# Attention on one NeuronCore: mixing on four array quadrants in the banks of the output, and another order of a round

## The reference, cut to what matters

```python
x = x + conv(group_norm(x))
x = x + attention(group_norm(x))

def attention(x):                       # n tokens, 8 heads of 16 channels
    q, k, v = x @ Wq.T, x @ Wk.T, 2 * (x @ Wv.T)
    q, k, v_h = l2norm(q), l2norm(k), l2norm(v)      # per head
    A = softmax(einsum('bnhd,bngd->bnhg', v_h, v_h))  # 8 x 8 per token, over g
    q = einsum('bnhg,bngd->bnhd', A, q)
    k = einsum('bnhg,bngd->bnhd', A, k)
    P = softmax(einsum('bnhd,bnhe->bnde', k, q))      # 16 x 16 per token, over e
    out = einsum('bnhd,bnde->bnhe', v, P)
    # transposed and reshaped to (n, 128), so that a row mixes tokens of one image
    return out @ proj_w.T + proj_b
```

## Time and profile before

| what | value |
|---|---|
| median of three runs | 3333.34 us |
| the profiled execution | 3327.52 us, span 3325.7 us |
| TensorE matmuls busy | 2987.1 us, 90% of the span |
| weight loads busy (beside matmuls) | 2207.7 us, 66% |
| VectorE, ScalarE, POOL busy | 1866.8, 1275.8, 570.3 us |
| mean granted TensorE clock | 0.955 |
| four attention bursts on the chain that ended last | logits 7%, mixing, scores and outputs 6% each |

### The profile page before, as it was taken

How to read it: one execution, slowest core, us unless ns; L and a number is a source line. 1 busy time by engine, 2 the same in 40 slices (tenths; PEclk the granted TensorE clock), 3 DMA queues, 4 the chain that set the end, 5 groups by cost and what they waited for, 6 DMA issues and landing times. The chain is left out here.

```text
span 3325.7 us, 143922 instructions
## 1 busy us (share of the span) xinstructions
PE 2987.1 (90%) x62769; PEld 2207.7 (66%) x62769; DVE 1866.8 (56%) x3334; ACT 1275.8 (38%) x2841; POOL 570.3 (17%) x419
## 2 busy tenths in 40 slices
PE   6686989999999999999998995889888898988897
PEld 5463369766666666666665443777777777777777
DVE  4452542566666666666665773555555555555553
ACT  3453552422222222222222443444444444444431
POOL 0000030022222222222221222111111111111111
PEclk8787889999999999999999996999999999999999
DMA  6877000021112121212114985555555555564551
GB/s 143 229 227 198 1 1 1 13 47 45 46 44 46 43 46 43 46 44 45 45 44 174 414 326 139 84 85 95 103 109 85 104 91 113 85 110 85 104 85 49
DMA packets 1015824, 318.88 MB, mean 96 GB/s; under 512 B 863345, under 2 KB 1002158, under 8 KB 1010350
## 3 DMA queue, kind: packets, MB, share of 16 engines
q1 hardware_dynamic: 692626, 169.81, 24.7%
q10 hardware_dynamic: 322844, 143.73, 15.8%
HBM read 157.66 MB, written 155.75 MB: 94 GB/s over the span
## 5 line engine op out<-in xcount | busy, mean ns | idle before, releaser
L845 DVE TENSOR_TENSOR terms<-spec,ps_z 112x456 f32<-112x456 f32 x1024 | 575.0, 623 | 404.4 <-PE ps_z L728 404.4
L738 PEld LDWEIGHTS ps_q<-inv_w,prod 112*57 112x57 f32 x16384 | 450.9, 133 | 174.6 <-issue 172.2
L738 PE MATMUL ps_q<-inv_w,prod 112*57 112x56 f32 x16384 | 484.4, 217 | 1.2 <-DVE prod L851 1.2
L826 POOL TENSOR_TENSOR prod<-terms 112x456 f32<-112x456 f32 x256 | 297.6, 1162 | 1000.6 <-DVE terms L845 1000.6
L728 PE MATMUL ps_z<-x_half,fwd_w 120*112 120x456 f32 x1024 | 458.4, 570 | 0.0
L783 ACT ACTIVATE q_half<-ps_q 121x448 f32<-121x448 f32 x255 | 138.9, 545 | 827.3 <-PE ps_y L746 827.3
L1131 POOL TENSOR_TENSOR k_blocks<-k_mixed,same_of 128x896 f32<-128x896 f32 x112 | 193.4, 1727 | 1071.2 <-ACT k_mixed L1274 1071.2
L1180 PE MATMUL ps_l<-q_mixed,k_blocks 32*64 32x64 f32 x12544 | 230.1, 220 | 66.4 <-issue 65.6
L1180 PEld LDWEIGHTS ps_l<-q_mixed,k_blocks 32*64 32x64 f32 x12544 | 205.3, 133 | 83.2 <-issue 75.2
L1157 PEld LDWEIGHTS ps_s<-v_blocks 128*64 128x64 f32 x6272 | 199.0, 141 | 90.0 <-issue 81.0
L728 PEld LDWEIGHTS ps_z<-x_half,fwd_w 120*112 120x112 f32 x1024 | 160.4, 176 | 121.9 <-issue 106.1
(11 more groups left out here) (140 smaller groups left out, 4340.0 us busy)
## 6 DMA issues: line engine op xcount, KB each, us to landing
qk_heads<-st_qk ACTq DMA_DIRECT2D x56, 476.0 KB, 4.6
qk_rows<-qk_heads SPq DMA_DIRECT2D x56, 476.0 KB, 6.8
conv_in<-v_sb ACTq DMA_DIRECT2D x112, 224.0 KB, 3.3
v_in<-conv_in SPq DMA_DIRECT2D x512, 49.0 KB
conv_out<-y_sb ACTq DMA_DIRECT2D x512, 49.0 KB
y<-conv_out SPq DMA_DIRECT2D x8, 1792.0 KB, 13.6
x_in<-in_x SPq DMA_DIRECT2D x8, 1568.0 KB, 9.5
shortcut<-short ACTq DMA_DIRECT2D x8, 1568.0 KB, 6.2
```

Source lines behind the costliest of these rows:

```text
L738: last = pe.matmul(ps_q[64 * ri:64 * ri + NF, c * SIDE:(c + 1) * SIDE], prod[b % 2][:, x, c * NF:(c + 1) * NF], k.inv_w[:, x, ri * SIDE:(r ...
L826: pool.tensor_tensor(prod[b % 2][:, 1, :], terms[b % 2][:, 2, :], terms[b % 2][:, 3, :], ALU.add).then_inc(prod_i_r, 1)
L845: last = dve.tensor_tensor(terms[b % 2][:, x, :], k.spec[0:NFFT, s, bass.ds(c * CC, CC), :].rearrange("p c f -> p (c f)"), ps_z[b % 2][z][ ...
```

## The change

- `mix` alternates: for odd groups the two row halves write the other partitions (`half = 64 * (a ^ g % 2)`), so that all four quadrants are used; even groups go to the first and odd groups to the second of two banks, `ps_mix_o`.
- The output of `outputs` goes to the first of these banks, columns 0 to 271; mixing uses columns 272 on of both. In odd groups the halves of a group are thus swapped from mixing to the logits and are swapped back in `outputs`, whose halves now come in the order 0, 1, 1, 0.
- Because of the shared bank, `mix(i)` waits for the evacuation of outputs(i - 3), and `outputs(i)` waits for q and k of mixing(i + 2), the mixing of the same round, to have left.
- TensorE's round becomes: mixing, projection, scores, final, outputs, projection, logits. ScalarE: root, `leave_mix`, `copy_in`, `exp_s`, `store_heads`, `copy_in`, `exp_l`, store. VectorE: weigh, mask, add_bias, leave, divide, squares, clamp, normalize.

The number of instructions and of bytes stays as it is. The diff, without two blank lines ahead:

```diff
...
     TB, BPB, GB, GU = 112, 4, 28, 14
     NB = BATCH * TOK // (TB * BPB)
     NU = 2 * NB
@@ -1037,6 +1039,8 @@
     NIN = 4
     RPI = TOK // 16
     RH = RPI // 2
+    MC = (GU + 3) * HD
+    MW = GU // 2 * QKM
     with ExitStack() as ctx:
         def sb(n, shape):
             return ctx.enter_context(nc.sbuf_tensor(n, shape, F32))
@@ -1066,7 +1070,8 @@
         oT = [sb(f"oT{m}", [128, HD, RPI]) for m in range(2)]
         x1 = sb("x1_in", [128, TOK])
         res = [sb(f"res{m}", [RH, 4, CH]) for m in range(4)]
-        ps_a, ps_m, ps_o, ps_f = (psum(n) for n in ("ps_qkv", "ps_mix", "ps_o", "ps_qkv_fin"))
+        ps_a, ps_f = (psum(n) for n in ("ps_qkv", "ps_qkv_fin"))
+        ps_mo = psum("ps_mix_o", (128, 2, 512))
         ps_s, ps_l = psum("ps_s", (128, 2, 512)), psum("ps_l", (128, 2, 512))
         xn_loaded = [sem(f"xn_loaded{m}") for m in range(3)]
         st_stored = [sem(f"st_stored{m}") for m in range(2)]
@@ -1163,10 +1168,13 @@
                 if i:
                     pe.wait_ge(q_r, i)
                     pe.wait_ge(km_r, i)
+                if i >= 3:
+                    pe.wait_ge(o_r, i - 2)
                 for g, gb in groups(i):
                     for a in range(2):
                         rows = slice(64 * a, 64 * a + 64)
-                        last = pe.matmul(ps_m[rows, g * QKM:g * QKM + 64], eb[i % 2][rows, g, :], strided(qk[n % NIN][rows], gb * QKW, [[1, 64]]), start=True, stop=True)
+                        half, at = 64 * (a ^ g % 2), MC + g // 2 * QKM
+                        last = pe.matmul(ps_mo[half:half + 64, g % 2, at:min(at + 64, 512)], eb[i % 2][rows, g, :], strided(qk[n % NIN][rows], gb * QKW, [[1, min(64, 512 - at)]]), start=True, stop=True)
                 last.then_inc(m_ps, 1)
 
             def logits(i):
@@ -1186,9 +1194,14 @@
                 pe.wait_ge(p_r, i + 1)
                 if i:
                     pe.wait_ge(o_r, i)
+                if unit(i + 2):
+                    pe.wait_ge(q_r, i + 3)
+                    pe.wait_ge(km_r, i + 3)
                 for g, gb in groups(i):
                     for a in range(2):
-                        last = pe.matmul(ps_o[64 * a:64 * a + 64, g * HD:g * HD + 64], vb[n % NIN][:, gb, a, :], pn[i % 2][:, a, g:g + 4, :], start=True, stop=True)
+                        r = a ^ g % 2
+                        last = pe.matmul(ps_mo[64 * r:64 * r + 64, 0, g * HD:g * HD + 64], vb[n % NIN][:, gb, r, :], pn[i % 2][:, a, g:g + 4, :],
+                                         start=True, stop=True)
                 last.then_inc(o_ps, 1)
 
             def final(b, u):
@@ -1211,22 +1224,23 @@
             scores(0)
             for i in range(ROUNDS):
                 bk = AHEAD * BPB + 2 * i
+                if unit(i):
+                    mix(i)
+                if bk < NB * BPB:
+                    project(bk)
                 if unit(i + 1):
                     scores(i + 1)
+                if i in FINS:
+                    final(*FINS[i])
                 if unit(i - 2):
                     outputs(i - 2)
-                if unit(i):
-                    mix(i)
-                if unit(i - 1):
-                    logits(i - 1)
-                if i in FINS:
-                    final(*FINS[i])
                 if bk < NB * BPB:
-                    project(bk)
                     if i in FINS:
                         b, u = FINS[i]
                         pe.wait_ge(f_r, b * 8 + u + 1)
                     project(bk + 1)
+                if unit(i - 1):
+                    logits(i - 1)
 
         @block.scalar
         def _(act):
@@ -1265,13 +1279,13 @@
                 act.activation(pe_[i % 2][:].rearrange("p r g e -> p r (g e)"), ps_l[:, :, 0:GU * HD], ACT.Exp).then_inc(l_exp, 1)
 
             def leave_mix(i):
-                ps = ps_m[:, 0:GU * QKM].rearrange("p (g x) -> p g x", x=QKM)
+                ps = ps_mo[:, :, MC:MC + MW].rearrange("p j (g x) -> p g j x", x=QKM)
                 act.wait_ge(m_ps, i + 1)
                 if i >= 2:
                     act.wait_ge(q_r, i - 1)
                     act.wait_ge(k_r, i - 1)
-                act.activation(dsq[i % 2][:], ps[:, :, HD:HD + 1], ACT.Square).then_inc(d_r, 1)
-                act.activation(km[i % 2][:], ps[:, :, HD + 1:], ACT.Copy).then_inc(km_r, 1)
+                act.activation(dsq[i % 2][:].rearrange("p (g j) x -> p g j x", j=2), ps[:, :, :, HD:HD + 1], ACT.Square).then_inc(d_r, 1)
+                act.activation(km[i % 2][:].rearrange("p (g j) x -> p g j x", j=2), ps[:, :, :, HD + 1:], ACT.Copy).then_inc(km_r, 1)
 
             def store(b, u):
                 act.wait_ge(f_r, b * 8 + u + 1)
@@ -1294,17 +1308,18 @@
                 bk = AHEAD * BPB + 2 * i
                 if i % 2 == 0 and i // 2 + AHEAD - 1 < NB:
                     root(i // 2 + AHEAD - 1)
+                if unit(i):
+                    leave_mix(i)
+                if bk < NB * BPB:
+                    copy_in(bk)
                 if unit(i + 1):
                     exp_s(i + 1)
                 if i % 2 == 1 and i // 2 + AHEAD - 1 < NB:
                     store_heads(i // 2 + AHEAD - 1)
-                if unit(i):
-                    leave_mix(i)
+                if bk < NB * BPB:
+                    copy_in(bk + 1)
                 if unit(i - 1):
                     exp_l(i - 1)
-                if bk < NB * BPB:
-                    copy_in(bk)
-                    copy_in(bk + 1)
                 if i in FINS:
                     store(*FINS[i])
             for m in range(4):
@@ -1343,14 +1358,15 @@
 
             def weigh(i):
                 a = i % 2
-                ps = ps_m[:, 0:GU * QKM].rearrange("p (g x) -> p g x", x=QKM)
+                ps = ps_mo[:, :, MC:MC + MW].rearrange("p j (g x) -> p g j x", x=QKM)
                 dve.wait_ge(d_r, i + 1)
                 dve.reciprocal(wgt[a][:], dsq[a][:]).then_inc(w_r, 1)
                 dve.wait_ge(w_r, i + 1)
                 dve.wait_ge(km_r, i + 1)
                 if i >= 2:
                     dve.wait_ge(l_ps, i - 1)
-                dve.tensor_tensor(qm[a][:, 0:GU, :], ps[:, :, 0:HD], wgt[a][:].to_broadcast([128, GU, HD]), ALU.mult).then_inc(q_r, 1)
+                dve.tensor_tensor(qm[a][:, 0:GU, :].rearrange("p (g j) d -> p g j d", j=2), ps[:, :, :, 0:HD],
+                                  wgt[a][:].rearrange("p (g j) x -> p g j x", j=2).to_broadcast([128, GU // 2, 2, HD]), ALU.mult).then_inc(q_r, 1)
 
             def divide(i):
                 a = i % 2
@@ -1369,7 +1385,7 @@
                 if i % UPI == 0 and b >= 2:
                     dve.wait_ge(f_ps, 8 * (b - 1))
                 n, g0 = i // 2, i % 2 * GU
-                dve.tensor_tensor(oT[b % 2][:, :, r0:r0 + GU].rearrange("p e g -> p g e"), ps_o[:, 0:GU * HD].rearrange("p (g e) -> p g e", e=HD),
+                dve.tensor_tensor(oT[b % 2][:, :, r0:r0 + GU].rearrange("p e g -> p g e"), ps_mo[:, 0, 0:GU * HD].rearrange("p (g e) -> p g e", e=HD),
                                   qk[n % NIN][:, g0:g0 + GU, QKM:QKM + 1].to_broadcast([128, GU, HD]), ALU.mult).then_inc(o_r, 1)
 
             def add_bias(b, u):
@@ -1391,16 +1407,16 @@
                         normalize(pr // 2 - 1)
             mask(0)
             for i in range(ROUNDS):
+                if unit(i):
+                    weigh(i)
                 if unit(i + 1):
                     mask(i + 1)
+                if i in FINS:
+                    add_bias(*FINS[i])
                 if unit(i - 2):
                     leave(i - 2)
-                if unit(i):
-                    weigh(i)
                 if unit(i - 1):
                     divide(i - 1)
-                if i in FINS:
-                    add_bias(*FINS[i])
                 pr = AHEAD * 2 + i
                 if pr < NB * 2:
                     squares(pr)
```

## The result

The changed kernel takes **3453.5 us** (median of 4 runs, 3448.44 to 3459.8) where the kernel before took 3334.73 beside it: ratio 1.035 [1.0325, 1.0379], 119 us slower. Slower was forecast; the forecast of 3359 and the range up to 3415 were too low by 94.5 and 38.5.

What follows compares the result with a forecast made beforehand. TensorE was taken to set the round, with 145 us lost to late instruction blocks. The new order's loop adds 96 us, instruction waits go from 145 to 75: +26 us, so 3359 us, range 3284 to 3415.

Steps and rivals of the forecast that it cites:

- Mixing on four quadrants: TensorE's mixing burst of 56 matmuls takes about 0.92 us instead of 1.78, a gain of 0.86 us per round if TensorE sets it.
- Rival 3: Mixing's burst stays at 1.78 us, outputs still wait and only the last eight rounds lose their gain: 3366 us; chance 0.05.
- Outputs in the order 0, 1, 1, 0: Outputs burst on TensorE: same 56 instructions in the new order of halves, cost 0, or 1.74 us more if overlap is lost.
- Rival 4: Outputs on TensorE lose their overlap, up to 1.74 us more in nearly every round, 181 us: 3540 us; chance 0.04.
- The loop: Outputs' wait for mixing's evacuation, with logits last, chains TensorE, VectorE and ScalarE: rounds of 11.9, 10.8, 9.15 and 10.75 us, sum +96.
- rival 2: ScalarE and VectorE reach mixing's evacuation earlier than their written order suggests, so TensorE's slots rule: 3211 to 3284 us; chance 0.05.
- 58 us for the last seven steps: Undisturbed time before the change of the seven steps left: five of 10.84 - 1.99 us and two of 8.51 - 1.48.
- Instruction waits: TensorE waits for blocks of 256 instructions, most in the logits: 145 us before the change, 75 left after, bounds 0 and 145.
- 17 for the rest: Of 162 us missing from the undisturbed rounds before the change, what was left for everything but late instruction blocks.
- Rival 1: New idle time on TensorE hides the instruction fetch; with all 145 us gone the kernel is 49 us faster, 3284; chance 0.22.
- POOL expands this round's k ... Cost 0: POOL's expansion of k, for the next round's logits, stays off the loop, a round ahead of its user: cost 0.
- the faster mixing is worth almost nothing either way: Conclusion on TensorE's mixing: even if its burst stays at 1.78 us the time is 3366 against 3359; the order decides.

## Why the prediction was wrong in size and right in direction

Step by step, in medians: before 3334, the order 3331, with the wait 3400, with shared banks 3405, with four quadrants 3453. (The runs come from several sets, in which the median of the kernel before lies between 3333 and 3338, so steps of a few us are no steps.)

- **Mixing on four quadrants**: right, a little less than counted. The slot is 0.96 for 1.78 at 2.4 GHz, a gain of 0.82 for 0.86. The sentence that was held against it, that a weight load overlaps running matmuls only when the row groups differ, stands in the Trainium skill (TensorE: Matmul & The Clock Gate) in the section "The mechanism", not in the one that the prediction names. What was drawn from it does not hold: with the same two row groups in the same order the rate nearly doubles once the column halves alternate too. Rival 3 is out.
- **Outputs in the order 0, 1, 1, 0**: right. An undisturbed burst has 1.78 from its start to the next one's (2606.22 to 2608.00). Rival 4 is out.
- **The loop**: right, and rival 2 is out. With POOL held back, the four kinds of round take 11.56, 11.04, 9.22 and 11.02. By the prediction's own sum (its 58 us for the last seven steps less 0.86 each, 52) that is 25.5 x 22.60 + 26.5 x 20.24 + 52 = 1165 us undisturbed, predicted 1062 + 96 = 1158: 7 more.
- **Instruction waits, and no term for the clock**: the size was off. That kernel's rounds took 1284.21 in all, which is 119 over the 1165, for the predicted 75 + 17 = 92: 27 more. The prediction put all that changes there down to instruction waits and kept 17 for the rest; it had no term for TensorE's clock, of which it said only that it is nearly always at 2.4 GHz. With POOL held back TensorE is at 1.2 GHz for 88.7 us of the rounds and before for 46.6, so by the estimate up to 20 of the 27 can be the clock; the runs don't divide them. Rival 1, faster by the fetch, is out: the rows of instruction waits add up to more than before. Its mechanism is there in part: without the loads of v the change gains 30 us where the kernel before gains 80, so waits ahead of the loop's wait cost little.
- **"POOL expands this round's k ... Cost 0"**: this step failed. The change's rounds took 1338.19, 54 more than with POOL held back (41 us more of them at 1.2 GHz are in this). The prediction asked whether POOL's result comes in time for the logits; it does. It didn't ask what else runs while POOL runs. The earlier trace rows have VectorE's part of the loop, with nothing from POOL beside it. Before, k_blocks started 1.94 us or more ahead of p_norm and was done when that began; in the new order with mixing on two quadrants it starts 0.65 or more behind; mixing's gain of 0.8 us puts it 0.1 ahead, so that p_norm waits for nearly all of it.

7 + 27 + 54 = 88 of the 94.5 us that were missing; the rest is time outside the rounds, of which the profiled execution of the changed kernel has 7 us more than that of the kernel before.

So the statement "the faster mixing is worth almost nothing either way" can hold only without the collision. With it, the same 0.8 us cost 48. That this cost comes from the collision and not from the fetch is shown by the kernel with POOL held back, whose mixing is just as fast.

The order, which the prediction held for the decisive part, is neutral; what decides is the wait that the shared banks force on it (69) and the collision (48 to 60), each with what comes with it in instruction waits and clock.

Open: what TensorE's clock costs by itself, why fetches stay late with the loads of v gone, and which instruction of a block asks for the next.

## What to carry to other kernels

When a step is made faster or moved, ask for every engine that it feeds what will then run at the same time, not only whether its result still comes in time: here an engine 16% busy put 1.4 us on a loop it isn't part of, in 31 rounds. A bank shared with this round's product ties the next burst to two other engines' written order, so count that loop before sharing. Where TensorE waits for its instructions, a shorter burst can gain nothing by itself: try slow matmuls between fast bursts. And read the granted clock of single bursts, not only its mean: a mean of 0.95 for 0.98 was 83 us more at 1.2 GHz.

## What the runs showed of the hardware

- VectorE's p_norm, a tensor_tensor with both inputs in SBUF, does not share with POOL's tensor_tensor but waits for its end: 2.03 to 2.15 us for 0.62, in all 31 rounds in which POOL (1.68) started up to 0.13 us earlier. The small copy to st_qk waits as well, 0.99 for 0.13 in the round below, ending at 2603.37 where POOL ends at 2603.32; the reciprocal rnorm ran beside the same expansion in its usual 0.74, and q_mixed, one input in PSUM, in its 0.39. From the timeline of the kernel after, POOL's and VectorE's:

```profile
2601.64 1.68 POOL L1136 TENSOR_TENSOR k_blocks<-k_mixed,same_of 128x896 f32<-128x896 f32 x1 [6.44 <-ACT k_mixed L1288]
```

```profile
2601.72 0.74 DVE L1342 RECIPROCAL rnorm<-nrm 112x96 f32<-112x96 f32 x1
2602.38 0.99 DVE L1345 COPY st_qk<-nrm 112x32 f32<-112x32 f32 x1
2603.27 1.28 DVE L1348 TENSOR_TENSOR st_qk<-qkv,rnorm 112x512 f32<-112x512 f32 x2
```

- It works in both directions: in the kernel with mixing on two quadrants, an expansion that started at 2586.41, 0.24 us after VectorE's first product for st_qk (0.69), took 1.99 us for 1.68.
- The Trainium skill has this (SBUF — State Buffer, "SBUF: two separate sides"): the port pair that VectorE and GpSimd share is an exclusive lock, taken for a whole instruction by whichever starts first of a GpSimd instruction and a VectorE one that has two SBUF inputs or runs in a 2-port mode. The trace agrees for two SBUF inputs, with the 2.05 above. The small copy has one, and no row shows in which mode it ran; its 0.99 fits the second case.
- TensorE's instruction supply is a limit that no engine's busy share shows: waits of 105.1 us before and 134.7 after, those over 0.5 us a multiple of 256 instructions apart. With a burst 0.80 us shorter per round the waits in the logits grew from 79.6 to 127.0 us and the kernel lost 14 us (3353 to 3366), a part of which can be the clock. Setting a projection between mixing and the logits, with the bias add early, gained 53 (3338 beside it, to 3285) with not one matmul changed.
- At the 1.2 GHz level small float32 matmuls lose nearly half their rate: outputs 3.21 us for 1.78, mixing 1.67 for 0.96.
